# First attention pass with swapped order and shifted upper scores, and an output projection in three bf16 products whose halves GpSimd splits

## The reference

```
term1 = einsum('bhqd,bhkd->bhqk', Q, K)
term2 = einsum('bhqd,kd->bhqk', Q, r)
term3 = einsum('hd,bhkd->bhk', u, K)[:, :, None, :]
term4 = einsum('hd,kd->hk', v, r)[None, :, None, :]
scores = (term1 + term3 + rel_shift(term2 + term4)) / sqrt(dk)
attn = softmax(scores, axis=-1)
out = einsum('bhqk,bhkd->bqhd', attn, V).reshape(B, S, H * dv)
return out @ Wo + bo
```

## Time and profile before

| | |
|---|---|
| median of 3 runs | 3898.95 us |
| the profiled execution | 3905.26 us, its span 3903.5 us |
| TensorE busy (share of the span) | 3371.7 us (86%) |
| VectorE | 2714.4 us (70%) |
| GpSimd | 1657.7 us (42%) |
| ScalarE | 1505.6 us (39%) |
| maxima, L849 | 1024 x 556 ns |
| selecting copies, L843 | 1024 x 364 ns |
| "never" matmuls, L926 | 512 x 341 ns |
| output projection, L1009 | 512 x 401 ns |

### The profile page before, as it was taken

The page is one execution under the profiler, slowest core; times in us unless marked ns, Lnnn a source line. Parts: engine busy times, 40 slices in busy tenths (PEclk is TensorE's granted clock), DMA queues, the critical chain, the costliest instruction groups (busy, mean ns, idle before and its releaser), DMA issues. The chain is left out here.

```text
span 3903.5 us, 92302 instructions
## 1 busy us (share of the span) xinstructions
PE 3371.7 (86%) x35174; PEld 2573.9 (66%) x35238; DVE 2714.4 (70%) x6150; ACT 1505.6 (39%) x2989; POOL 1657.7 (42%) x2049
## 2 busy tenths in 40 slices
PE   6999996799999999999995501899399999998996
PEld 5888885577777777777772200677267667675765
DVE  5888885577777777777765787455166666665876
ACT  3444442255555555555562300322033333332221
POOL 2555554265665666666660100477400000004776
PEclk9999998599999999999997855899699999998998
DMA  4666664555555554654635400444233333225775
GB/s 137 189 193 194 191 192 146 112 151 137 138 149 132 147 147 125 152 147 125 154 97 163 141 0 3 111 120 126 92 108 105 117 105 107 95 87 143 202 197 143
DMA packets 450401, 519.32 MB, mean 133 GB/s; under 512 B 63917, under 2 KB 419979, under 8 KB 449572
## 3 DMA queue, kind: packets, MB, share of 16 engines
q1 hardware_dynamic: 428552, 474.63, 42.9%
q0 software_dynamic: 21504, 39.94, 3.8%
HBM read 308.37 MB, written 215.94 MB: 134 GB/s over the span
## 5 line engine op out<-in xcount | busy, mean ns | idle before, releaser
L849 DVE TENSOR_REDUCE p_mx<-p_psS 98x2 f32<-98x392 f32 x1024 | 527.6, 556 | 0.0
L843 DVE COPY_PREDICATED p_psS<-p_later,p_psD 98x198 f32<-98x198 uint32 (+1 forms) x1024 | 325.5, 364 | 250.6 <-PE p_psD L926 250.6
L794 ACT ACTIVATE p_after<-p_psF 98x392 f32<-98x392 f32 x512 | 255.0, 498 | 589.5 <-PE p_psF L939 579.8
L797 ACT ACTIVATE p_probs<-p_psE 98x392 f32<-98x392 f32 x1024 | 450.1, 496 | 0.0
L743 POOL TENSOR_SCALAR_AFFINE_SELECT p_after<-p_after 98x392 f32<-98x392 f32 x512 | 275.1, 537 | 358.0 <-ACT p_after L794 348.5
L1284 POOL COPY sb_wt<-sb_gw 112x8 f32 (+1 forms) x28 | 7.2, 257 | 760.5 <-DMA sb_gw<-scratch_gw 760.4
L747 POOL TENSOR_SCALAR_AFFINE_SELECT p_probs<-p_probs 98x392 f32<-98x392 f32 x512 | 275.0, 537 | 112.3 <-ACT p_probs L797 104.4
L1290 POOL DMA_INDIRECT sb_ye<-scratch_ye,sb_idx x224 | 246.1, 1099 | 83.0 <-issue 59.1
L962 PE MATMUL p_psO<-p_probs,p_v 98*32 98x196 f32 x4096 | 279.1, 344 | 1.8 <-POOL p_probs L747 1.7
L1274 POOL DMA_INDIRECT scratch_xe<-sa_xs,sa_idx x224 | 220.0, 982 | 116.9 <-issue 76.8
L419 POOL TENSOR_TENSOR p_rt<-p_rt 128x784 f32<-128x784 f32 x64 | 187.1, 2924 | 122.6 <-DVE p_st L397 122.6
(11 more groups left out here) (287 smaller groups left out, 10439.5 us busy)
## 6 DMA issues: line engine op xcount, KB each, us to landing
scratch_stack<-p_st SPq DMA_DIRECT2D x64, 784.0 KB, 6.0
p_x<-in_x SPq DMA_DIRECT2D x32, 1176.0 KB
p_L<-scratch_stack SPq DMA_DIRECT2D x192, 196.0 KB, 4.3
p_U<-scratch_stack SPq DMA_DIRECT2D x192, 196.0 KB, 4.5
scratch_xe<-p_zero SPq DMA_DIRECT2D x32, 1024.0 KB, 5.5
ex_xin<-scratch_xe SPq DMA_DIRECT2D x64, 512.0 KB, 4.0
scratch_ye<-ex_y SPq DMA_DIRECT2D x64, 512.0 KB, 2.8
scratch_h<-p_h SPq DMA_DIRECT2D x32, 392.0 KB
```

Of the source, the lines that this page charges most:

```text
L794: act.activation(after[c][:].rearrange("p h t -> p (h t)"), psF[:, 0:4 * TILE], ACT.Exp, scale=DK ** -0.5).then_inc(p_ok.sem, 1)
L797: act.activation(probs[c][:, b, :], psE[:, b, 0:PAIR], ACT.Exp, scale=DK ** -0.5).then_inc(p_ok.sem, 1)
L843: nc.vector.copy_predicated(own[:, :, c * TILE:c * TILE + wide], later[:, 0:wide].unsqueeze(1).broadcast_to([TILE, 2, wide]), upper).then_ ...
L849: nc.vector.tensor_reduce(mx[g1][:, c, 4 * q1 + 2 * b:4 * q1 + 2 * b + 2], own, AX.X, ALU.max).then_inc(s_max.sem, 1)
```

## The change

It has two parts.

First, `stage_s`. The upper scores now read the keys one column further on (`mid.start + 1`), so that their columns are the keys beyond the query by one place, and they are written first, ahead of the scores. In the second half only 97 keys are left, and a matmul of 4 columns (an identity times the constant `outside`, -1e28) fills the last column of each head. The "never" matmul is gone, and with it its table; the scores of the first half leave out the last column, and so do the maxima there. VectorE's copy of each pair of heads waits for this pair's bank alone (`3 * c + b + 2`), where both waited for the last matmul of the position (`3 * c + 3`).

Second, the projection. GpSimd splits the quotient into `attn16`, a bf16 half and a bf16 remainder (a cast and a subtraction, each waiting by `attn_parts` for the instruction before it), and once, ahead of the values, the weights into `woh` and `wol`. TensorE transposes four bf16 blocks instead of two fp32 ones, and multiplies in three products (high by high, high by low, low by high) for each half of the 256 rows. ScalarE copies four blocks instead of two.

```diff
-        attnT = sb("attnT", [128, 2, TILE])
+        attn16 = sb("attn16", [TILE, 2, C], BF16)
+        attnT = sb("attnT", [128, 2, 2, TILE], BF16)
+        woh, wol = (sb(x, [128, 2, C], BF16) for x in ("woh", "wol"))
...
+        wo_split, attn_parts = semaphore(nc, ctx, "p2_wo_split"), signal("attn_parts", 4)
...
                         nc.gpsimd.tensor_tensor(attn[:], num[:], rden[:].unsqueeze(2).broadcast_to([TILE, HEADS, DK]),
-                                                           ALU.mult).then_inc(attn_ok.sem, 1)
+                                                           ALU.mult).then_inc(attn_parts.sem, 1)
+                        flat = attn[:].rearrange("p h d -> p (h d)")
+                        pool.wait_ge(attn_parts.sem, attn_parts.at(k - 1, 2 * t + 1))
+                        nc.gpsimd.tensor_copy(attn16[:, 0], flat).then_inc(attn_parts.sem, 1)
+                        pool.wait_ge(attn_parts.sem, attn_parts.at(k - 1, 2 * t + 2))
+                        nc.gpsimd.tensor_tensor(attn16[:, 1], flat, attn16[:, 0], ALU.subtract).then_inc(attn_ok.sem, 1)
 
                 pool.wait_ge(setup, 16 * 2)
+                nc.gpsimd.tensor_copy(woh[:], wo[:]).then_inc(wo_split, 1)
+                pool.wait_ge(wo_split, 1)
+                nc.gpsimd.tensor_tensor(wol[:], wo[:], woh[:], ALU.subtract).then_inc(wo_split, 1)
...
-                        act.activation(attnT[:], psM[:, 0:2 * TILE].rearrange("p (h t) -> p h t", h=2), ACT.Copy).then_inc(att_ok.sem, 1)
+                        act.activation(attnT[:].rearrange("p a b t -> p (a b t)"), psM16[:, 0:4 * TILE], ACT.Copy).then_inc(att_ok.sem, 1)
...
-                        wide = TILE + 1 - c
-                        dve.wait_ge(s_ok.sem, s_ok.at(s1, 3 * c + 3))
                         for b in range(2):
                             own = psS[:, b, 0:PAIR].rearrange("p (h t) -> p h t", h=2)
-                            upper = psD[:, 2 * wide * b:2 * wide * (b + 1)].rearrange("p (h t) -> p h t", h=2)
-                            nc.vector.copy_predicated(own[:, :, c * TILE:c * TILE + wide],
-                                                      later[:, 0:wide].unsqueeze(1).broadcast_to([TILE, 2, wide]),
+                            upper = psD[:, 2 * TILE * b:2 * TILE * (b + 1)].rearrange("p (h t) -> p h t", h=2)
+                            dve.wait_ge(s_ok.sem, s_ok.at(s1, 3 * c + b + 2))
+                            nc.vector.copy_predicated(own[:, :, c * TILE:(c + 1) * TILE],
+                                                      later[:].unsqueeze(1).broadcast_to([TILE, 2, TILE]),
                                                       upper).then_inc(chosen.sem, 1)
                         for b in range(2):
-                            own = psS[:, b, 0:PAIR].rearrange("p (h t) -> p h t", h=2)
+                            own = psS[:, b, 0:PAIR].rearrange("p (h t) -> p h t", h=2)[:, :, 0:S - 1 + c]
...
+                    pe.wait_ge(chosen.sem, chosen.at(s, 2) if c else chosen.at(s - 1))
+                    wide = TILE - c
+                    for j in range(4):
+                        h = 4 * q + j
+                        last = nc.tensor.matmul(psD[:, j * TILE:j * TILE + wide], U[u][0:STACK, h][:, mid],
+                                                K[u][0:STACK, h][:, mid.start + 1:mid.start + 1 + wide], start=True, stop=True)
+                    if c == 1:
+                        last = nc.tensor.matmul(psD[:, 0:4 * TILE].rearrange("p (h t) -> p h t", h=4)[:, :, TILE - 1], ident16[:], outside[:],
+                                                start=True, stop=True)
+                    last.then_inc(s_ok.sem, 1)
                     for b in range(2):
...
-                    wide = TILE + 1 - c
-                    pe.wait_ge(chosen.sem, chosen.at(s, 2) if c else chosen.at(s - 1))
-                    for j in range(4):
-                        h = 4 * q + j
-                        nc.tensor.matmul(psD[:, j * wide:(j + 1) * wide], U[u][0:STACK, h][:, mid],
-                                         K[u][0:STACK, h][:, mid.start:mid.start + wide], start=(j == 0), stop=False)
-                    upper = psD[:, 0:4 * wide].rearrange("p (h t) -> p h t", h=4)
-                    nc.tensor.matmul(upper[:, :, 1:wide], ident16[:], beyond[:, :, 0:wide - 1], start=False, stop=True).then_inc(s_ok.sem, 1)
...
-                            for j in range(2):
-                                last = nc.tensor.matmul(psM[0:TILE, 0:C], attnT[:, j, :], wo[:, j, :],
-                                                        start=(j == 0), stop=(j == 1))
+                            pe.wait_ge(wo_split, 2)
+                            last = three_products(nc, psM[0:TILE, 0:C], [
+                                (attnT[:, 0, j, :], attnT[:, 1, j, :], woh[:, j, :], wol[:, j, :]) for j in range(2)])
```

More of the change, by code:

```diff
@@ L538, in attend @@
         ident16 = sb("ident16", [TILE, TILE], BF16)
-        never32, never = (sb(x, [TILE, NEVER_COLUMNS], dt) for x, dt in (("never32", F32), ("never", BF16)))
-        beyond = never[:, 2 * (TILE + 1):2 * (TILE + 1) + TILE].unsqueeze(1).broadcast_to([TILE, 4, TILE])
-        later = sb("later", [TILE, TILE + 1], U32)
+        never32 = sb("never32", [TILE, NEVER_COLUMNS])
+        outside = sb("outside", [TILE, 4], BF16)
+        later = sb("later", [TILE, TILE], U32)
         wo, bo = sb("wo", [128, 2, C]), sb("bo", [TILE, C])
@@ L914, in stage_s @@
                                 nc.tensor.matmul(out[:, 0:TILE], low[:, mid], key[:, first:second], start=True, stop=True)
-                                last = nc.tensor.matmul(out[:, TILE:S], up[:, mid], key[:, second:second + TILE], start=True, stop=True)
+                                last = nc.tensor.matmul(out[:, TILE:S - 1], up[:, mid], key[:, second + 1:second + TILE], start=True, stop=True)
                             else:
@@ L1000, in position @@
                                 pe.wait_ge(mrow_ok.sem, mrow_ok.at(k + 1))
[L1001 to L1004 removed]
+                            for part in range(2):
+                                for j in range(2):
+                                    at = (2 * part + j) * TILE
+                                    last = nc.tensor.transpose(psM16[:, at:at + TILE], attn16[:, part, 128 * j:128 * j + 128], ident16[:])
                             last.then_inc(at_ok.sem, 1)
```

10 lines of the change are left out of this document (3 added, 7 removed).

## The result

| | before | changed |
|---|---|---|
| median | 3898.54 us (3896.86 to 3908.42, 4 runs) | 3846.40 us (3841.79 to 3849.52, 4 runs) |
| ratio | | 0.986 (0.9841 to 0.9879) |
| the profiled execution | 3905.26 us | 3845.78 us |
| one image of the steady state | 20.69 us | 19.69 us |

The account below looks back on a forecast made before the run. TensorE's own work, or waits it runs into, bounds the attention stage. 60.4 (steady state) + 8 (head) - 1.5 (tail) gives 67 less than 3905.26, 3838; the median, 6 lower, gives 3832 us, range 3775 to 3895.

Parts of the forecast that it names:

- the steady state: Attention stage at full clock: 61 images, each 19.70 us instead of 20.69, together 60.4 us less.
- the head: Start of the attention stage: twelve positions at 1.2 GHz, 2.91 us each falling to 2.0; 10.9 less, taken as 8.
- the tail: End of the attention stage: two GpSimd chains lie bare, 2 x (1.03 - 0.29), 1.5 us more.
- the walk: One image followed through the engines with the new durations: waits sum to 2.06 us, image 19.62, before 0.08 was added.
- Rival B: Waits don't add up: only the stall at the quotient remains, 18.5 us per image, 3759 us; chance 0.10.
- The never matmul: TensorE's first pass: 0.17 us gone in 8 positions, 1.36 per image, less 0.2 for four four-column matmuls.
- The order: Upper scores first, copies waiting for their own pair: nearly no waits left in a plain position, TensorE's 1.80 us the bound.
- Rival C: Hand-over between TensorE and VectorE not freed: 1.4 us of waits stay, 3869 us, or 3906 with dearer GpSimd instructions; chance 0.14.
- The sign that I had named for it: VectorE's total wait for the upper scores should fall below 50 us from 250.
- The projection: Six bf16 matmuls instead of four fp32 on TensorE: 0.66 us instead of 0.95, 0.58 less per image.
- GpSimd's chain: Quotient, cast and subtraction with two waits of 0.05 between them: 1.65 us where one instruction took 0.62.
- Rival D: Slower through GpSimd's added work: 3950 us at 0.95 per new instruction, 4020 at 0.82 per wait for itself; chance 0.14.

Follow-up runs that it names:

- the first pass alone: Changed kernel with GpSimd's cast and subtraction and the bf16 products taken back, so the FP32 projection as before; 3772.4 us, 0.9667 of before.
- chain alone: FP32-projection kernel with the new stage_s, plus GpSimd's cast and subtraction behind each division, results unused, transposes waiting for them; 3865.6 us, 0.9905 of before.
- the subtraction behind the masks: Changed kernel with GpSimd's subtraction issued after the next position's masks and the first quotient's transposes after the following first pass; 3895.3 us, 0.9981 of before.
- the transposes later: Changed kernel with only TensorE's transposes of the first quotient moved behind the next position's first pass; 3815.4 us, 0.9781 of before.

## Why the prediction was right, and where it was not

The forecast of 3832 missed by 14 us. The sum was -60.4 for the steady state, -8 for the head and +1.5 for the tail. In the two traces, from the first second-pass scores to the last copy of the max rows, it was (1970.9 - 725.3) - (2032.5 - 726.7) = -60.2; up to there -1.4; from there to the end of the stage +10.0. That is 15 short of the forecast, and head and tail are the whole of it. The unchanged stages behind took 7.9 less in the profiled executions, about as much as they differ between the other kernels, so that these two are 59 us apart; the medians are 52 apart, near what the three parts of the stage give.

- **The steady state, 19.70 for 19.69.** It is right term by term, each to within 0.2 us, and what they are off cancels to 0.01, which is luck. The measure is the prediction's own, from a matmul's start to the next one's. Positions take 1.80 and 1.84, as forecast. With 0.48, 0.18 and 0.70 at the ends of positions, each twice, 0.18 for the maxima's transposes, and the output matmuls that are 0.12 shorter ahead of these, TensorE's own work is some 17.4, where 17.56 was taken. The waits are the other 2.3, where 2.06 + 0.08 was taken: 1.11 at the transposes (0.97), 0.56 for the masks (0.40), and about 0.6 for maxima (0.10, 0.30 and 0.23). The waits for maxima stand where the walk had them, behind the maximum chain and one position on. The first of them, TensorE's timeline:

```profile
1635.25 0.79 PE L937 MATMUL p_psS<-p_K,p_L 96*98 96x196 bf16 x4
1635.88 0.35 PE L951 MATMUL p_psF<-p_U,p_K 98*98 98x98 bf16 x4
```

  The second pass starts 0.63 after the scores, where it is 0.35 from 1620.61 to 1620.96. The second wait is 0.24, in the scores that begin behind 1637.22, and no list of waits has it. Nor does the busy time of 18.05 us an image measure own work: it counts a matmul to its end, and these scores are drawn out, 0.79 for 0.52. Rival B, 18.5 an image, has both stalls and these waits against it.
- **The never matmul,** 1.16 net per image. Taken out by itself it was worth 1.19, of which 0.96 reached the period. The four-column matmul costs 0.03, where 0.05 was taken.
- **The order** frees the hand-over: 1.05 us an image by itself. Rival C is refuted: the changed kernel's weight loads wait 14.8 us for maxima between 900 and 1900, where it was 74.7 before, and the run that puts the old order back has those waits again. The sign that I had named for it was wrong, though: VectorE's wait for scores did not fall below 50 us, it is 185 us (250 before). Part of those waits now follows TensorE's stalls: behind the one at the transposes VectorE stands idle for 1.28 us, until the first scores are there. The step missed that a stall of TensorE is written down as a wait of VectorE too; at 101.5 us the wait is smaller in the first pass alone.
- **The projection,** 0.58 an image. It takes 0.70 where 0.66 was taken, from 0.95: 0.50. The quotient's transposes, whose change was put at nothing, went from 0.23 to 0.18 (1630.02 to 1630.20), some 0.08 an image, so that the 0.58 came out by luck. Of it only 0.30 reached the period, as the rest became waits for maxima.
- **GpSimd's chain,** taken at 1.65, is 1.84: cast 0.40 (0.31), subtraction 0.67 (0.62), the two waits for itself 0.07 and 0.08 (0.05). Rival D's upper rows (0.95 an instruction, 0.82 a wait) don't apply. Its price of 12 us for each 0.1 us holds nowhere: 1.22 us of chain cost 93 us, 8 for each 0.1 (chain alone), the subtraction's 0.74 were worth 51, 7 for each 0.1, with new waits beside them, and the second subtraction's 0.63 cost 200, 32 for each 0.1, with the clock at 0.90. That the clock can fall the prediction had only as a last sentence. Kernels in which it falls can't be placed by adding up waits alone.
- **The head, 8 predicted, 1.4 found.** The step that failed is "so 10.9 less", cut to 8 for one wait of 0.60. The positions did run in 2.0 us each and the max rows were ready at 711.80 in place of 718.92. But the step was followed to VectorE's copy only, and not into SyncE's queue, where the second pair's loads stood ahead of the max rows' transfers. Before the change these loads were issued by 715.04, ahead of the max rows at 719.27, and cost nothing. Now the queue is free only at 714.45, and the max rows' own issue takes 4.01 us (1.20 before). With the loads put behind, 9.2 us appear.
- **The tail, +1.5 predicted, +10 found.** Priced as two bare chains at full clock. In the last image there is no first pass to fill TensorE, its stall for the masks at 1973.29 is 1.75 us, and the clock went to 0.75 and 0.74 for 20 us; before the change it stayed at 1.00 up to 2050. The kernel with the chain alone has the same long tail, 44 us from the last max rows to the last residual add, against 32 in the kernel with the first pass alone and 32 before.

So the case for the change rests on its first part. The second is a loss of 74 us that the forecast had inside its own sum and never set out as a term: 0.58 gained, against 0.97 + 0.40 and their followers lost. Adding up by part, rather than by engine, would have shown it.

## What to carry to other kernels

Price each part of a change as if it came alone: a sum that is right as a whole can hide a part that loses. Cheap work on an idle engine isn't free when the busiest engine reads its result soon: here 1.2 us of GpSimd work, twice per image, cost 1.3 us an image, to save 0.3. And follow a result that comes earlier through the queue that carries it away, up to the instruction that needs it.

## What the runs showed of the hardware

- Stalls and the clock. TensorE kept 1.00 through stalls of 1.04 and 0.50 us in every 19.7 us, and had 0.90 on average with 1.66 and 1.13 in every 22.8. Single stalls of 1.62 (transfers) and 1.75 us (masks) were followed by more than 10 us at 1.2 GHz (0.50) and by 20 us at 0.75. But in the kernel with the subtraction behind the masks the clock fell behind many stalls of 0.93 us, and behind others of the same length it stayed at 1.00. So the length of a stall alone doesn't decide, and what does isn't settled by these runs. The Trainium skill (TensorE: Matmul & The Clock Gate, HAM oscillation) describes a clock that waits between bursts bring down again and again; these rows agree, with waits of 0.93 to 1.75 us that are shorter than those of its example.
- Where the clock falls a wait costs more than itself: 1.25 us of added stall went with 3.09 us of added period.
- A VectorE instruction can last as long as one of GpSimd beside it. In the maximum chain it was the first instruction, with a median of 479 ns over all images; now that one has 220, and the second is the long one. Here it is at the head, and what GpSimd did:

```profile
706.59 1.18 DVE L869 TENSOR_SCALAR p_nm<-p_mf 98x32 bf16<-98x32 f32 x1
```

```profile
706.47 1.26 POOL L740 TENSOR_TENSOR p_h<-p_h,p_bo 98x512 f32<-98x512 f32 x1
```

  They end within 0.04 us of each other, at 707.77 and 707.73. Over all images the second's median went from 181 to 430 ns. So the wait changed its place more than its size, and the 0.08 that the prediction added for more of it did not come as such. The second reads one tile; the rule of the Trainium skill that the prediction cites (GPSIMD Engine Reference, Specifications) speaks of a performance mode or two SBUF inputs, and whether this instruction ran in such a mode no row shows.
- Transfers of the max rows can become TensorE's next wait: 0.2 us in 1000 with the changed kernel, 24.1 and 9.1 with images of 19.18 and 18.68 us, and none with 19.21 (the transposes later). What sets them apart is open; no kernel here changed these transfers in the steady state.
